# The second group's token scatters all issued in steps 29 and 30, none in the expert slots

## The reference

```
K, V, Q = x @ theta_K.T, x @ theta_V.T, x @ theta_Q.T
per token: g = 2/512 * (W @ k + b - v); W -= 0.01 * outer(g, k); b -= 0.01 * g; out = W @ q + b
x = layernorm(x + out)
shared = silu(x @ sW1 + sb1) @ sW2 + sb2
act = sqrt(softplus(x @ routing_W.T + expert_bias)); the 2 largest of 8 experts, weighted by act
y = shared + sum over the 2 experts of act_e * (silu(x @ rW1[e] + rb1[e]) @ rW2[e] + rb2[e])
x = layernorm(x + y)
```

## Time and profile before

| what | us |
|---|---|
| median of 3 runs | 2340.74 (2336.39 to 2342.3) |
| the profiled execution's own time | 2332.68 |
| its span in the profile | 2330.9 |
| PE busy | 2200.8 (94%) |
| DVE busy | 1524.9 (65%) |
| POOL busy | 1218.7 (52%) |
| ACT busy | 916.8 (39%) |

### The profile page before, as it was taken

How to read it: one execution, slowest core, us unless ns; L and a number is a source line. 1 busy time by engine, 2 the same in 40 slices (tenths; PEclk the granted TensorE clock), 3 DMA queues, 4 the chain that set the end, 5 groups by cost and what they waited for, 6 DMA issues and landing times.

```text
span 2330.9 us, 40319 instructions
## 1 busy us (share of the span) xinstructions
PE 2200.8 (94%) x12738; PEld 1905.5 (82%) x12738; DVE 1524.9 (65%) x3794; ACT 916.8 (39%) x2136; POOL 1218.7 (52%) x1168
## 2 busy tenths in 40 slices
PE   8999999999999999999999999997889789999896
PEld 6888888888888888888888888885778678888775
DVE  5666666666666776666666676664354336887798
ACT  4333333334334333433333433331444335544444
POOL 1345534445433336665455532465556565777667
PEclk9999999999999999999999999998899899999998
DMA  4212222111221111222111110008333225887896
GB/s 169 73 64 73 82 87 77 64 66 71 82 87 51 37 37 40 71 82 86 51 37 41 42 55 28 29 19 354 112 111 119 94 92 182 294 289 240 284 328 215
DMA packets 112203, 257.18 MB, mean 110 GB/s; under 512 B 21618, under 2 KB 23282, under 8 KB 109056
## 3 DMA queue, kind: packets, MB, share of 16 engines
q1 hardware_dynamic: 83776, 187.35, 22.9%
q0 software_dynamic: 27936, 67.22, 8.8%
q10 hardware_dynamic: 288, 0.04, 0.0%
HBM read 160.36 MB, written 105.26 MB: 114 GB/s over the span
## 4 chain that ended last, share of the span: by engine, by line
PE 47%; DVE 8%; issue 5%; ACT 2%; POOL 2%; another core or an unknown queue 1%; DMA 1%; DVEq 1%; SPq 0%; ACTq 0%; POOLq 0%
PE banks L114 14%; PE banks L116 14%; PE banks L115 13%; PE banks L763 2%; PE banks L120 2%; DVE b_Y L1138 1%; DVE b_XL L1135 1%; DVE b_small L1690 1%; PE banks L790 1%; DVE b_Y L1135 1%; DVE b_HL L1135 1%; POOL W L1747 1%; PE banks L505 1%; DVEq L1655 1%
## 5 line engine op out<-in xcount | busy, mean ns | idle before, releaser
L114 PE MATMUL banks<-W 128*128 128x512 f32 (+1 forms) x2040 | 743.3, 364 | 14.5 <-DVE W L1135 7.6
L116 PE MATMUL banks<-W 128*128 128x512 f32 (+1 forms) x2040 | 717.9, 352 | 0.0
L115 PE MATMUL banks<-W 128*128 128x512 f32 (+1 forms) x2040 | 717.6, 352 | 0.0
L114 PEld LDWEIGHTS banks<-W 128*128 128x128 f32 x2040 | 388.3, 190 | 59.7 <-DVE W L1135 7.5
L116 PEld LDWEIGHTS banks<-W 128*128 128x128 f32 x2040 | 387.1, 190 | 54.3
L115 PEld LDWEIGHTS banks<-W 128*128 128x128 f32 x2040 | 388.4, 190 | 42.4
L1747 POOL TENSOR_TENSOR W<-S,W 128x512 fp32r<-128x512 f32 (+1 forms) x249 | 321.0, 1315 | 137.8 <-ACT W L834 137.2
L834 ACT ACTIVATE W<-banks 128x512 fp32r<-128x512 f32 x320 | 189.8, 594 | 345.4 <-PE banks L116 140.1
L1747 POOL TENSOR_TENSOR X<-X,B 128x1024 f32<-128x1024 f32 x32 | 76.9, 2404 | 421.7 <-DMA X<-in_x 421.6
L834 ACT ACTIVATE W<-S 128x512 fp32r<-128x512 f32 (+1 forms) x256 | 161.8, 654 | 213.7 <-DVE S L1135 207.3
L1135 DVE TENSOR_TENSOR W<-banks,W 128x512 fp32r<-128x512 f32 x192 | 132.3, 689 | 152.2 <-ACT W L834 152.2
(11 more groups left out here) (171 smaller groups left out, 4434.8 us busy)
## 6 DMA issues: line engine op xcount, KB each, us to landing
RG<-ys SPq DMA_DIRECT2D x128, 256.0 KB
XT<-in_xT SPq DMA_DIRECT2D x32, 512.0 KB
X<-in_x SPq DMA_DIRECT2D x32, 512.0 KB
x1d<-X SPq DMA_DIRECT2D x64, 256.0 KB
wd<-RG SPq DMA_DIRECT2D x32, 512.0 KB, 3.9
W<-wd SPq DMA_DIRECT2D x16, 1024.0 KB, 13.1
out<-b_Y SPq DMA_DIRECT2D x64, 256.0 KB
zd<-X SPq DMA_DIRECT2D x52, 256.0 KB, 2.0
```

What stands on the lines that cost most here:

```text
L114: e.matmul(o, ll, rh, start=start, stop=False, skip_group_check=True)
L115: e.matmul(o, lh, rl, start=False, stop=False, skip_group_check=True)
L116: return e.matmul(o, lh, rh, start=False, stop=stop, skip_group_check=True)
```

## The change

The table now gives the second group's 24 tiles to two steps, 12 tiles and so 24 scatters in each, in place of 8 tiles each and 8 left over. From step 26 on, nine scatters (if there are so many) stand ahead of `xb(t)` in place of one. The places behind `xb(t)` stay. So steps 29 and 30 issue 9, 3, 1, 1, 6 and 4 scatters in the places named above (before: 1, 3, 1, 1, 6 and 4), and slots 2 to 17 issue none (before: one each). In step 26 both scatters of the first group's last tile stand ahead of `xb`.

```diff
-SCATTERS = [[3] * 10, [8, 8]]
+SCATTERS = [[3] * 10, [12, 12]]
...
         scattered = scatters(t)
-        next(scattered, None)
+        for _ in range(9 if t >= k.groups[-1]["step"] else 1):
+            next(scattered, None)
         xb(t)
         next(scattered, None)
         next(scattered, None)
```

## The result

The change measures 2331.38 us (median of 12 runs, 2325.14 to 2334.16) against 2341.70 us for the kernel before (12 runs, 2336.39 to 2345.36): ratio 0.9954, 95% interval 0.9943 to 0.9966. That is 10.3 us faster. The forecast was 2321.0 us, 10 us too low, with a range of 2311 to 2334 us that holds the result.

A forecast was written before the change was run, and what follows sets the result against it. PE was taken to bound the kernel, scatters in slots 2 to 17 making it wait: 20.3 us won less 0.4 for steps 29 and 30 takes 2332.68 to 2312.8, plus 8.06 to the median gives 2321 us, range 2311 to 2334.

The forecast's parts named there:

- The gain in the slots: Slots 2 to 17 without scatters fall from 5.10 to 3.84 us a slot: 20.3 us won.
- its signs for the slots: Sends of slots 2 to 18 in 61 to 66 us, PE idle under 6 us, slots 36 to 59 still 5.1 us.
- the rival of a partial share: Slots 2 to 17: table loads and DVE routing keep part, 72.1 us, only 11.8 won, 2329 us; chance 0.12.
- "does nothing" rival: Waits in slots 2 to 17 only coincide with scatters; slots keep 5.2 us, total 2341 us; chance 0.04.
- The runs of nine: Steps 29 and 30: eight more scatters each ahead of `xb` take 10.1 us, hidden in POOL's idle time.
- For the 16 I take 16 x 0.025 = 0.4 us: Price of the 16 scatters added in steps 29 and 30, at 0.025 us each: 0.4 us.
- no wait for `ids` in POOL's runs of nine: Sign for steps 29 and 30: POOL's scatters ahead of `xb` never wait for an older one's landing.
- The sign for DVE's addition: DVE's addition to X stays within 0.3 us of its place in steps 29 and 30.
- the landings: Rival: landings pace steps 29 and 30's runs at 2.72 us a scatter, 28.1 us lost, total 2348.5 us; chance 0.06.
- The sum: Whole kernel: 20.3 - 0.4 = 19.9 us off the profiled execution, median some 2321 us.

The follow-up runs named there:

- the pairs: The change, but eight of step 30's nine front scatters go in four pairs, each behind a wait for DVE: 2313.91 us, ratio 0.9905 where before takes 2335.34.
- the powers: The change plus two small POOL powers (some 1.3 us), no DMA, in each of slots 18 to 35: 2320.67 us, ratio 0.9950 where before takes 2335.34.

## Why the prediction was right or wrong

- **The gain in the slots: right, and right in size.** 20.3 us were forecast; 17.9 by `b_Y` and 22.3 by sends came, 18.4 in the pairs. All its signs for the slots held: 61.6 us between the sends (61 to 66), PE's idle 4.2 us (under 6), the rival of a partial share would have shown 72.1 us. (That rival counts DVE's routing steps in 14 of the slots 2 to 17; there are 12, and its sum would be 71.3.) Slots 36 to 59 stayed, at 124.84 / 24 = 5.20 us (5.1).
- **The reading of it holds on the slow kind alone.** That a scatter is what makes a slot slow was a difference of stretches, and the prediction said that it could name no chain. On the quick kind the same scatter costs POOL 0.44 us a slot of lag and PE nothing. There the "does nothing" rival is what happened, for a reason it didn't have: the kernel has no wait there to take away. On the slow kind the reading rests on the stretches and on taking the scatters out, three times (65.4, 64.9 and 63.4 us in place of 83.3); no chain from a scatter to PE's wait was found there either.
- **The runs of nine: right on POOL, wrong on the rest of the core.** The step that failed is "For the 16 I take 16 x 0.025 = 0.4 us". It looked for the price in POOL's queue: lateness of `xb` and of POOL ahead of the roots. POOL was late for neither (`xb` 1560.7 forecast, 1561.74 come; an idle of 13.74 us ahead of step 30's root), and the landings let the run go at 1.27 us, with two small waits in step 29, against the sign "no wait for `ids` in POOL's runs of nine". What broke is that DVE and ACT take PE's products late while POOL issues DMAs without a break, here 13 in a row, and PE idles 6.7 us. Term by term: 9.1 us in place of about 0.2 for step 30; in step 29 nothing (the root at +1.2 us, as step 28's). The sign for DVE's addition failed in both steps, by 1.2 us in step 29 (1516.22 for 1515.06, from ahead of it) and by 10.3 us in step 30, 9.1 of them within the step.
- **The base.** A steady-state price of 0.025 us, from intervals where scatters stood apart, was carried to a run the trace of before doesn't contain. The prediction saw that gap ("no run longer than five is in the trace") but set it against the landings only. And its rows held the five that stand there already, but it never added the eight to them: the run in step 30 is of 13, not nine.
- **The sum.** 19.9 forecast; in the profiles 17.9 won, 9.1 + 1.2 + 1.9 paid up to the slots, 3.2 lost behind: 2.5. By medians 10.3, by the pairs' medians 21.4: with step 30 mended the forecast's size is about met. That the result lies in the range is in part luck: the range's upper half was meant for a gain that is smaller in the slots, not for one that step 30 gives back, and on the quick kind nothing would have been won.

## What to carry to other kernels

When queue work is moved under another engine's cover, look at what it does to the others while it runs, not only at whether its own queue is on time. On the slow kind the safer form was software DMA issues in short runs with other work between them; and count what already stands ahead of the run. A pace between two issues of one engine is not the pace of the kernel where buffers lie between; cut stretches by the work that all engines share. And a gain that is a wait removed exists only where that wait exists: measure it on more than one chip.

## What the hardware showed that was not expected

- The same program takes 2248 us on some chips and 2335 to 2342 us on others, with steps of the same length (root to root 52.05 and 52.07 us in before), the difference being almost all in the second part (83.3 against 56.1 us in slots 2 to 17, with PE idle 16.6 against 0; 69.4 against 62.9 in slots 18 to 35, 122.0 against 83.7 in slots 36 to 59, 411.3 against 399.0 behind). The granted clock in slots 2 to 17 is 0.92 against 1.00, and PE's idle comes with it; which of the two is first, and what differs between the chips, is open.
- On the slow kind, DVE and ACT started late on PE's products in step 30, near the end of a run of POOL's indirect DMAs at 1.27 us. In both profiles with that run PE stopped about when the tenth issue went out (at 1555.0 with the tenth at 1554.61, and at 1553.7 with the tenth at 1554.04). The one profile with the run taken apart shows no such lateness. The nine of step 29 went without, but waits for landings cut them into pieces of four and less, so nine without a break were not seen. By what path the issues reach the others is not shown. A path that no run tests is the fetching of instructions: one packet of 16 KB of the instruction queue moves at this time in each profile, at 1553.2 us before, at 1554.8 and 1554.0 with the pairs and the powers, and only at 1558.4 in the late step of the change; it can be late as the cause or because the engines were.
- A scatter of 128 integers with one in flight goes at 2.40 us, with two at 1.27 us, the issue's own pace; with SP's weights in flight at 2.72 us. But with two in flight a landing now and then is later than 2.53 us: every profile with the nine of step 29 has two such waits, of 0.4 to 2.3 us. The Trainium skill, page "DMA: Bandwidth & Descriptors", section "Latency and other measured facts", puts the fixed cost of a DMA at some 2 us; this case's 2.40, which begins with the start of the issue, lies 0.4 us above it.
- PE's wait costs more than its length. After the idle of 4.21 us the granted clock from 1562.0 to 1565.5 is 0.50, the lower level of 1.2 GHz, and matmuls of 512 columns start every 0.43 us in place of 0.23. Over the whole step 30, before and after (root to root), PE does the same 267 matmuls, but idles 9.3 us in place of 2.9 and is busy for 51.92 us in place of 49.13, at a granted clock of 0.89 in place of 0.97.
